# One power for two norms' deviations, and five of a group's eight scatters behind TensorE signals

## The reference, cut to what matters

```python
x = x + tanh(g_xattn[0]) * attention0(layernorm(x), ctx)    # 16 heads
x = x + tanh(g_ffn[0])   * mixture0(layernorm(x))           # 6 experts, dense, weights of the best two
x = x + tanh(g_xattn[1]) * attention1(layernorm(x), ctx)    # one head
x = x + tanh(g_ffn[1])   * mixture1(layernorm(x))           # 8 experts, only the best two of a token
```

## Time and profile before

| | us |
|---|---|
| median of 3 runs | 872.78 |
| lowest and highest | 869.91, 873.79 |
| time of the profiled execution | 876.62 |
| its span, first to last instruction | 874.8 |
| TensorE busy in it | 769.0 (88%) |
| VectorE, ScalarE, GpSimd busy | 672.8, 555.9, 462.9 |

### The profile page before, as it was taken

How to read it: one execution, slowest core, us unless ns; L and a number is a source line. 1 busy time by engine, 2 the same in 40 slices (tenths; PEclk the granted TensorE clock), 3 DMA queues, 4 the chain that set the end, 5 groups by cost and what they waited for, 6 DMA issues and landing times. The chain is left out here.

```text
span 874.8 us, 26065 instructions
## 1 busy us (share of the span) xinstructions
PE 769.0 (88%) x8321; PEld 592.6 (68%) x8321; DVE 672.8 (77%) x2969; ACT 555.9 (64%) x1195; POOL 462.9 (53%) x498
## 2 busy tenths in 40 slices
PE   4999999999999978999899898777689988899992
PEld 2566666666666655677667666466679888788891
DVE  3789898898988877888788787854568565578893
ACT  2677777777778646788878877635446444444450
POOL 3445534455445301247777777666455556566564
PEclk9999999999999989999999999977989999999995
DMA  9100010000100000001111111121223332257764
GB/s 251 54 24 24 22 42 21 21 21 21 41 22 0 3 27 15 11 23 49 44 53 42 47 50 47 37 62 53 53 68 92 91 81 77 79 171 206 218 189 126
DMA packets 59173, 56.36 MB, mean 64 GB/s; under 512 B 9975, under 2 KB 49176, under 8 KB 59080
## 3 DMA queue, kind: packets, MB, share of 16 engines
q1 hardware_dynamic: 41736, 33.16, 14.0%
q0 software_dynamic: 8416, 17.38, 6.0%
q10 hardware_dynamic: 8928, 4.70, 1.9%
HBM read 32.65 MB, written 22.56 MB: 63 GB/s over the span
## 5 line engine op out<-in xcount | busy, mean ns | idle before, releaser
L1221 POOL DMA_INDIRECT contributions<-v_heads,d_token x135 | 132.9, 985 | 89.3 <-PE bc_bank L1979 42.6
L1205 POOL DMA_INDIRECT sorted_rows<-r_send,r_slots x128 | 126.6, 989 | 46.2 <-issue 41.2
L1962 PE MATMUL bc_bank<-d_xT,d_w 128*128 128x128 f32 x608 | 88.6, 291 | 21.8 <-DVE d_xT L1463 9.6
L1962 PEld LDWEIGHTS bc_bank<-d_xT,d_w 128*128 128x128 f32 x608 | 78.9, 202 | 26.7 <-DVE d_xT L1463 23.8
L504 POOL TENSOR_SCALAR a_k_heads<-a_kT,first 128x512 f32<-128x512 f32 x60 | 93.2, 1572 | 0.8 <-ACT a_kT L557 0.8
L1463 DVE COPY d_xT<-bc_bank 128x128 f32<-128x128 f32 x135 | 38.3, 284 | 68.5 <-PE bc_bank L1979 53.4
L422 DVE TENSOR_REDUCE a_neg_max<-a_scores 128x16 f32<-128x1024 f32 x64 | 78.1, 1221 | 10.6 <-PE a_scores L673 9.2
L581 ACT ACTIVATE a_probs<-a_scores 128x1024 f32<-128x1024 f32 x64 | 65.6, 1025 | 30.7 <-PE a_scores L683 30.6
L1725 ACT COPY d_w<-w 128x512 f32 x135 | 83.5, 618 | 2.0 <-issue 1.3
L588 ACT COPY a_probsT<-a_probsT_bank 128x512 f32<-128x512 f32 x128 | 74.8, 584 | 14.3 <-PE a_probsT_bank L700 13.8
L700 PE MATMUL a_probsT_bank<-first,a_probs 128*128 128x128 f32 x512 | 81.0, 282 | 2.2 <-ACT a_probsT L588 0.3
(11 more groups left out here) (236 smaller groups left out, 1997.7 us busy)
## 6 DMA issues: line engine op xcount, KB each, us to landing
d_rows<-sorted_rows SPq DMA_DIRECT2D x135, 65.0 KB
X<-in_x SPq DMA_DIRECT2D x16, 256.0 KB, 3.1
b_hidden<-contributions SPq DMA_DIRECT2D x8, 512.0 KB
b_weighted<-contributions SPq DMA_DIRECT2D x8, 512.0 KB
out_x<-X ACTq DMA_DIRECT2D x16, 256.0 KB
ctxT<-in_ctx_T SPq DMA_DIRECT2D x16, 192.0 KB, 3.0
c_ctxT<-in_ctx_T SPq DMA_DIRECT2D x16, 192.0 KB
contributions<-v_heads,d_token POOLq DMA_INDIRECT x135
```

The lines of the kernel that those rows point to most:

```text
L1205: pool.indirect_dma_start(dispatch.rows, bass.IndirectOffsetOnAxis(ap=slots[n % 2][:, k, j:j + 1], axis=0), send[n % 2][k][:, j, :], None) ...
L1221: pool.indirect_dma_start(dispatch.contributions, bass.IndirectOffsetOnAxis(ap=token[:, t % KEEP:t % KEEP + 1], axis=0), shares[t % KEEP], ...
L1962: last = pe.matmul(uv(m)[:, bass.ts(i, P)], w12[m % W12][:, bass.ts(i, P)], xT[m % TURNED][:], start=True, stop=True)
```

## The change

The `b_` and `c_` norms' variances and their inverse deviations now lie side by side in two shared tiles, `c.variances` and `c.rstds` (128 x 2 x 4). POOL raises both with one instruction of 128 x 8 values after it has waited for both variances, and then makes `ln`'s offset. In the steps where only one of the two groups exists, that one is done alone as before.

Five scatters get a wait in front: scatter 1 for the scores of group `i-4` (the same step's, on PE), scatter 3 for the values of group `i-4` (the same step's), scatter 4 for the transposes of `c_xn` of group `i-3` (PE's step `i+1`), scatter 5 for the ranks of group `i-5` (PE's step `i+1`), and scatter 7 for the mixture's output of group `i-2` (PE's step `i+1`; of the last group where there is none).

```diff
 class LayerNorm:
-    def __init__(self, name, sb, sem, c, X, own_rows=True, offsets=True):
+    def __init__(self, name, sb, sem, c, X, own_rows=True, offsets=True, half=None):
...
-        self.variance = sb(f"{name}_variance", [P, GT], F32)
+        self.variance = sb(f"{name}_variance", [P, GT], F32)[:] if half is None else c.variances[:, half]
...
-        self.rstd = sb(f"{name}_rstd", [P, GT], F32)
+        self.rstd = sb(f"{name}_rstd", [P, GT], F32)[:] if half is None else c.rstds[:, half]
...
-            def deviation1(n):
-                if within(n):
-                    ln1.deviation(pool, n)
+            def both_deviations(n, n1):
+
+                if not within(n):
+                    if within(n1):
+                        ln1.deviation(pool, n1)
+                    return
+                if not within(n1):
+                    ln.deviation(pool, n)
+                    ln.offset(pool, n)
+                    return
+                pool.wait_ge(ln.stats_done, n + 1)
+                wait_alone(pool, ln1.stats_done, n1 + 1)
+                pool.tensor_tensor(c.rstds[:], c.variances[:], c.minus_half[:].unsqueeze(1).broadcast_to([P, 2, GT]),
+                                   ALU.pow).then_inc(ln1.rstd_done, 1)
+                wait_alone(pool, ln1.rstd_done, n1 + 1)
+                pool.tensor_tensor(ln.minus_mean[:], ln.negated[:], ln.rstd, ALU.mult).then_inc(ln.offset_ready, 1)
...
-            def scatter(n, which):
-                if within(n):
+            def scatter(n, which, behind=None):
+                if within(n):
+                    if behind is not None:
+                        wait_alone(pool, *behind)
...
             for i in STEPS:
                 spread_deviation(ln2, i - 5)
-                scatter(i - 6, (0, 1))
-                deviation1(i - 3)
-                scatter(i - 6, (2, 3))
-                spread_deviation(ln, i + 1)
-                scatter(i - 6, (4,))
+                scatter(i - 6, (0,))
+                scatter(i - 6, (1,), (s_mm, i - 3))
+                both_deviations(i + 1, i - 3)
+                scatter(i - 6, (2,))
+                scatter(i - 6, (3,), (v_mm, i - 3))
+                scatter(i - 6, (4,), (xn1_transposed, i - 2))
                 number_rows(i - 5)
-                scatter(i - 6, (5, 6, 7))
+                scatter(i - 6, (5,), (ranks_mm, i - 4))
+                scatter(i - 6, (6,))
+                scatter(i - 6, (7,), (y_mm, min(i - 1, G)))
```

More of the change, by code:

```diff
@@ L264, in spread_of @@
             dve.tensor_scalar(self.negated[:], self.stats[:, :, 0], -1.0, None, ALU.mult)
-        dve.tensor_scalar(self.variance[:], self.stats[:, :, 1], EPS, None, ALU.add).then_inc(self.stats_done, 1)
+        dve.tensor_scalar(self.variance, self.stats[:, :, 1], EPS, None, ALU.add).then_inc(self.stats_done, 1)
     def deviation(self, pool, n):
         wait_alone(pool, self.stats_done, n + 1)
-        pool.tensor_tensor(self.rstd[:], self.variance[:], self.c.minus_half[:], ALU.pow).then_inc(self.rstd_done, 1)
+        pool.tensor_tensor(self.rstd, self.variance, self.c.minus_half[:], ALU.pow).then_inc(self.rstd_done, 1)
     def offset(self, pool, n):
         wait_alone(pool, self.rstd_done, n + 1)
-        pool.tensor_tensor(self.minus_mean[:], self.negated[:], self.rstd[:], ALU.mult).then_inc(self.offset_ready, 1)
+        pool.tensor_tensor(self.minus_mean[:], self.negated[:], self.rstd, ALU.mult).then_inc(self.offset_ready, 1)
     def rows(self, dve, n):
@@ L996, in mixtures_and_attention @@
     weighted = [sb(f"b_weighted{i}", [P, C0, GW], F32) for i in range(2)]
-    ln1 = LayerNorm("c", sb, sem, c, X, offsets=False)
+    ln1 = LayerNorm("c", sb, sem, c, X, offsets=False, half=1)
     ctxT = [sb(f"c_ctxT{i}", [DC + 1, GW], F32) for i in range(2)]
@@ L2045, in build @@
         load_constants(nc, sb, sem, c, a, dispatch)
-        c.ln = LayerNorm("b", sb, sem, c, X)
+        c.variances, c.rstds = sb("variances", [P, 2, GT], F32), sb("rstds", [P, 2, GT], F32)
+        c.ln = LayerNorm("b", sb, sem, c, X, half=0)
         for phase, args in ((attention_of_layer0, (c, a, X, dispatch)), (mixtures_and_attention, (c, a, X, dispatch, out))):
```

## The result

The changed kernel takes 890.25 us in the median of 4 runs (889.01 to 894.27), beside 873.28 (869.91 to 875.43) for the kernel before on the same chip. The ratio is 1.0205 with a 95% interval of 1.0179 to 1.0231: slower by about 2%, where 868.3 was forecast.

What follows compares the result with a forecast made beforehand. The prediction took a ring of handovers through POOL, with TensorE's signals held by scatters, to bound the fused loop. Its terms +1.0 - 1.7 - 2.0 - 1.8 = -4.5 took 872.78 to 868.3 us, range 861 to 877.

Steps and rivals of the forecast that it cites:

- What bounds the kernel: Fused loop: no engine full; handovers through POOL set the pace, ACT idling 1.05 us for offset after scatter 7.
- The signals are late because of scatters: Fused loop: TensorE's signals are held while scatters are processed; scores 0.84 us late, `mix` 2.0, against 0.04 without scatters.
- only the power counts: Rival for the fused loop: scatters hold nothing, waits change only order; 872.0 us, within a shared chance of 0.28.
- The joint power: One power of 1.87 us replaces two of 1.04 on POOL: list 0.2 us shorter per step, three early steps +1.0.
- the signs of being wrong: Fused loop: `c_xn` transposes late because scatter 3 moves to the second power's place (unpriced), or signals late as before.
- The waits themselves: Five waits on POOL: 0 to 1.5 us a step, taken as 0, since a wait already met costs nothing.
- Scatter 1 behind the scores: Full steps (7 to 15): scatter 1 frees the scores' signal; of TensorE's 3.5 us at `c_shifted`, half goes: -1.7 us.
- Scatter 7 behind `mix`: Full steps: scatter 7 starts 0.1 us after `mix`, `r_rstd` earlier, ACT waits 0.5 us less in 4 steps: -2.0 us.
- theory C: From the experiments, not the prediction: scatter 4 waiting for the transposes delays POOL's list, 2 us each step.
- The late steps: After step 15: scatters 5 to 7 behind ranks and `mix` free 7.0 us; POOL's delay costs 5.2; net -1.8 us.
- Slower: Rival, chance 0.17: signals are late by themselves and a queue now stands behind scatter 7; 880 us, range 875 to 883.
- What would show it: Right: scatter 7 0.1 us after `mix`, steps of 15.9 to 16.1; wrong: ACT idle over 1.05 before `r_send` every step.

Runs made afterwards that it cites:

- e13: The changed kernel, but `r_send` waits only for scatters 0 to 3 of the group two before, whose buffer half it overwrites: 1.0171 of the kernel before.
- e9: The kernel before with one wait more, scatter 1 behind the scores: 0.9993 of the kernel before.
- e1: The changed kernel with the joint power in its new place and none of the five waits: 1.0262 of the kernel before.
- e8: The changed kernel without the waits of scatters 1, 3, 4 and 7, so joint power and scatter 5's wait: 1.0093 of the kernel before.
- e3: The changed kernel without the wait of scatter 7 for the mixture's output: 0.9993 of the kernel before.
- e5: The changed kernel without waits and with two separate powers, both at the joint power's place: 1.0236 of the kernel before.
- e7: The kernel before with one wait more, scatter 7 behind the mixture's output: 1.0043 of the kernel before.
- e16: The kernel before with scatter 1's wait from step 7 and those of scatters 3, 4 and 5 from step 15, powers apart: 0.9910 of the kernel before.
- e4: The changed kernel without the wait of scatter 4 for the transposes: 1.0112 of the kernel before.
- e10: The kernel before with one wait more, scatter 5 behind the ranks: 0.9992 of the kernel before.
- e11: The kernel before with the waits of scatters 1, 3, 4 and 5 from step 15 on, powers apart: 0.9958 of the kernel before.
- e12: The changed kernel with the two powers apart at their old places up to step 6: 1.0190 of the kernel before.
- e15: The changed kernel with `r_rstd` ahead of scatter 7 in POOL's list, `r_send` still waiting for all eight scatters: 1.0451 of the kernel before.

## Why the prediction was wrong

**What bounds the kernel: right for the change, not for the kernel before.** In the change and in e13 it is `r_send`, released behind scatter 7, that sets the pace. That it did so before is not borne out. In e9 both waits that were priced for the full steps are gone from 400 to 530 us, ACT's 3.6 us for `r_send` and TensorE's 3.5 for `c_shifted`, and `r_rstd` comes 3.7 to 4.0 after the start of `mix` in all nine steps 7 to 15, earlier than the 4.1 forecast. Yet the nine take only 0.8 us less together (144.7 for 145.5), where -1.7 and -2.0 were taken. In the waits of e9 from 400 to 530 us TensorE stands for something else, which it hardly waited for before:

```profile
PE bc_bank L1858 <- DVE r_chosen L1444: 3.0, 5, 0.8
```

One wait was also not read. That `r_send` waits for scatter 7 to land shows in the waits of before, 400 to 530 us, only as little, beside the 3.6 for POOL, and the prediction missed it:

```profile
ACT r_send L285 <- DMA sorted_rows<-r_send,r_slots: 0.5, 2, 0.2
```

**The signals are late because of scatters: right.** e1 against e8 shows it best: the same powers at the same place, and wait 5 alone, which moves only scatters 5 to 7 and what follows them, takes 1.7 points off (the four waits of e3 take 2.7). The Trainium skill ("SBUF — State Buffer", section Who interferes with whom) has it that TensorE and ScalarE never wait on anyone, in a list on access to SBUF. The prediction drew from it, which the page does not say, that scatters hold nothing and only the power counts, about 872 us; e1, which is 2.6% slower than before, does not bear that out, and the measurement decides. Whether the page's sentence itself holds here, no run shows. How a scatter holds a signal stays open, and not every scatter does (see scatter 6 below).

**The joint power: its size right, its place missed.** 1.67 us measured, 1.87 taken. The early steps lost 0.8 us where 1.0 was taken, and step 6 another 1.0 (17.12 against 16.12). But "POOL's list gets shorter by 0.2" left out that the second power had stood between two groups of scatters: without waits its place costs 2.4% (e5), 21 us. Only the signs of being wrong name it, unpriced (scatter 3 moves to where the second power stood). This second failed step was hidden in the whole change because the waits put gaps back into the train (e1 against e3).

**The waits themselves: a wrong row.** "A wait already met costs nothing" came from `r_rstd` and held: scatter 5 with its wait met (433.07) starts 0.15 behind the numbers, as it does in e1 without a wait (429.22). For unmet waits I took 0.1 us from signal to scatter; it is 0.75 (e9) to 0.79 (e7).

**Scatter 1 behind the scores: the signal came free, the gain did not.** -1.7 taken; alone -0.1% with an interval that holds both signs (e9). `c_neg_max` is within 0.3 of the scores in the full steps, as predicted, and these gain 0.1 each (e16).

**Scatter 7 behind `mix`: the step that failed.** It was to bring `r_rstd` to 4.1 us behind the start of `mix` in every step, worth -2.0. It brought it to 5.8 in five of the nine steps 7 to 15, and with waits 1, 3, 4 and 5 in place the wait costs 2.1 points (e3). In the step shown, `mix` takes 2.92, scatter 7 starts 1.87 later, and its 0.96 and 0.02 follow. Of the 1.87, 0.75 is what a scatter takes that had to wait (e9). The other 1.1 I read as the signal held by scatter 6, which runs over the end of `mix` (434.36 to 435.32); that is not shown. In the next step scatter 6 (451.90 to 452.86) runs over the end of `mix` too (452.60), and scatter 7 starts only 0.80 after that end.

The condition that the prediction named, scatters 2 to 6 following each other as before, did not hold. In the slow steps scatter 4 waits for the transposes (431.61), and scatters 5 and 6 come behind it, 1.1 and 2.4 us after the start of `mix`. Where scatter 5 waits for the ranks instead (450.61, 0.93 after it), `r_rstd` comes at 4.7. Without wait 4 that is so in seven of the nine steps (e4). So wait 4, more than wait 5, is what makes wait 7 dear, and theory C had a part of it; why 0.2 us decide is open. Not even a signal on time would have gained: 2.92 + 0.79 + 0.98 is 4.7, the worse of the two values before. The ring that this closes, `mix`, scatter 7, `r_rstd`, `r_send`, TensorE's transposes of it and all that follows in TensorE's order to the next `mix`, takes 17.3 to 17.7 us in the full steps of e13 and of the change in which `r_rstd` is 5.8 behind or more and the clock is full.

**The late steps: right.** The `c_rec` waits went. Alone wait 5 gives nothing that can be told (e10), with its neighbours and only there 0.4% (e11); -1.8 us taken, -3.7 measured there. In the change itself the last three steps take 2.6 less.

**The rivals.** "Slower" had the right end and nearly the right place (a queue behind scatter 7, `r_send` late), with 880 us instead of 890; it took the signal to be late by itself, and what was found is POOL's own start of 0.75 and 1.1 more in the slow steps. The joint power's place and the landing have a price in no rival. "What would show it" named ACT idle for over 1.05 us before `r_send` in every step, and that is what the trace shows (1.1 to 3.4 in the steps 7 to 15).

**Not settled: the half clock.** Two stretches of 10.2 us are in the change, and their steps took 5.1 and 6.8 us more than the same steps before: 11.9 of the 18.3 lost in the full steps. But e3, which has no loss, has two as well; and e13 has only 3.4 us of it before 560 and takes 11.2 us more than before in its full steps all the same, so the ring alone is enough for most of a loss of this size. In the full steps of the change, e3, e12 and e15 each such stretch began within 3 us after TensorE had waited 0.8 us or more for `r_send`. The reverse does not hold: waits of 1.74 at 426.4 and 1.56 at 467.3 in e15, and of 1.68 at 531.8 in e12, were followed by none, so what decides is open.

## What to carry to other kernels

Before a wait is put in front of an instruction, list what stands behind it in its queue and also who waits for its transfer to land; both lead back to the same engine here, and cutting one of them alone gained nothing that can be told, or made it worse, and a transfer that is moved pushes what now stands behind it. An idle time on another engine is worth only what the bounding engine gets of it: in e9 two waits of 3.6 and 3.5 us went, and 0.8 us were gained. Removing an instruction from between transfers is a change of their spacing: price the train that it leaves, not only the time that it saves. Pace only the transfers that nothing on the path waits for, and only in the steps where the trace shows a signal held.

## What was not expected of the hardware

A scatter that had to wait starts 0.75 us after VectorE has already acted on the same signal, against 0.30 behind another scatter. With a train of six scatters running, the signal of the transposed weights reached ScalarE 4.96 us after their modelled end, 1.1 us past the end of the train (e1). And TensorE stayed at 1.2 GHz for 10.2 us in which it was busy throughout (404.8 to 415.0), after an idle time of 1.07.
